# Bit patterns of each edge joined, the first weight product in quarters, residual sums on VectorE

## The reference

```python
# block 0
edge_feature = silu(edge_rbf @ We1 + be1) @ We2 + be2
msg = edge_feature * x[dst]
agg = segment_sum(msg, src, num_segments=625)
x = x + (x0 + (silu(agg @ Wn1 + bn1) @ Wn2 + bn2))   # x0 = max(layernorm(x), 0)
# block 1, on h = max(layernorm(x), 0)
h = relu(h @ W_init.T)
for l in range(3):           # mean over the edges of each node, both directions
    fwd = mean_agg(h, src, dst) @ W_fwd[l].T
    bwd = mean_agg(h, dst, src) @ W_bwd[l].T
    h = relu(concat(h, fwd, bwd) @ W_self[l].T)
# blocks 2 and 3: graph convolutions with 1/sqrt(degree) weights and dense layers
```

## Time and profile before

| | us |
|---|---|
| median of three runs | 1182.57 |
| profiled execution, its own time | 1181.72 |
| its span, first to last instruction | 1180.0 |
| PE busy | 1148.7 (97%) |
| DVE busy | 854.8 (72%) |
| ACT busy | 676.1 (57%) |
| POOL busy | 431.0 (37%) |

### The profile page before, as it was taken

How to read it: one execution, slowest core, us unless ns; L and a number is a source line. 1 busy time by engine, 2 the same in 40 slices (tenths; PEclk the granted TensorE clock), 3 DMA queues, 4 the chain that set the end, 5 groups by cost and what they waited for, 6 DMA issues and landing times.

```text
span 1180.0 us, 20814 instructions
## 1 busy us (share of the span) xinstructions
PE 1148.7 (97%) x6238; PEld 960.3 (81%) x6238; DVE 854.8 (72%) x1479; ACT 676.1 (57%) x1351; POOL 431.0 (37%) x546
## 2 busy tenths in 40 slices
PE   6999999999999999999999999999899999999998
PEld 3678887778888888888888888888879889897786
DVE  8898578877777777777777777777888325165665
ACT  3576665667667676766667676766734223141353
POOL 2002566766565655655565555553000000002000
PEclk9999999999999999999999999999999999999999
DMA  8623622222222222222222322222101203022101
GB/s 262 269 82 146 222 83 71 69 67 85 70 87 71 87 76 80 84 72 87 69 87 69 89 69 86 73 82 59 45 1 37 72 1 107 0 73 72 45 1 45
DMA packets 26966, 95.87 MB, mean 81 GB/s; under 512 B 6533, under 2 KB 6783, under 8 KB 22578
## 3 DMA queue, kind: packets, MB, share of 16 engines
q0 software_dynamic: 18592, 54.42, 15.5%
q1 hardware_dynamic: 8208, 40.84, 9.8%
q10 hardware_dynamic: 130, 0.13, 0.0%
HBM read 86.52 MB, written 8.85 MB: 81 GB/s over the span
## 4 chain that ended last, share of the span: by engine, by line
PE 74%; DVE 12%; ACT 7%; issue 4%; DMA 1%; POOL 1%; DVEq 0%; ACTq 0%; POOLq 0%
PE ps L1021 11%; PE ps L1022 11%; PE ps L1023 11%; PE ps L1014 8%; PE ps L1016 8%; PE ps L1015 8%; PE ps L1128 3%; PE ps L1127 3%; PE ps L1029 3%; PE ps L1028 3%; PE ps L1067 2%; ACT s L723 2%; PE ps L1132 2%; DVE msg L1696 1%; ACT s_hi L727 1%
## 5 line engine op out<-in xcount | busy, mean ns | idle before, releaser
L1021 PE MATMUL ps<-we_hi,s_hi 128*128 128x512 f32 x664 | 268.8, 405 | 0.0
L1022 PE MATMUL ps<-we_lo,s_hi 128*128 128x512 f32 x664 | 259.9, 391 | 0.0
L1023 PE MATMUL ps<-we_hi,s_lo 128*128 128x512 f32 x664 | 259.9, 391 | 0.0
L585 POOL DMA_INDIRECT xg<-h_dram,node_picks x166 | 177.1, 1067 | 96.2 <-POOL node_picks L575 65.6
L733 ACT ACTIVATE m_hi<-msg 128x512 fp32r<-128x512 f32 x166 | 105.0, 632 | 186.4 <-DVE msg L1696 185.0
L579 POOL DMA_INDIRECT rbf<-in_edge,edge_picks x166 | 175.1, 1055 | 50.5 <-issue 38.7
L1689 DVE TENSOR_TENSOR s_lo<-s,s_hi 128x1024 fp32r<-128x1024 f32 x83 | 101.6, 1225 | 78.3 <-ACT s_hi L727 78.3
L1701 DVE TENSOR_TENSOR m_lo<-msg,m_hi 128x512 fp32r<-128x512 f32 x166 | 114.7, 691 | 60.0 <-ACT m_hi L733 60.0
L1023 PEld LDWEIGHTS ps<-we_hi,s_lo 128*128 128x128 f32 x664 | 124.7, 188 | 27.6
L1021 PEld LDWEIGHTS ps<-we_hi,s_hi 128*128 128x128 f32 x664 | 125.0, 188 | 22.8
L1022 PEld LDWEIGHTS ps<-we_lo,s_hi 128*128 128x128 f32 x664 | 125.3, 189 | 20.6
(11 more groups left out here) (297 smaller groups left out, 2474.8 us busy)
## 6 DMA issues: line engine op xcount, KB each, us to landing
fold_dram<-folded SPq DMA_DIRECT2D x6, 1024.0 KB, 4.9
wstage<-fold_dram SPq DMA_DIRECT2D x6, 1024.0 KB, 4.8
plain<-in_fold_a SPq DMA_DIRECT2D x3, 1024.0 KB, 9.4
plain<-in_fold_b SPq DMA_DIRECT2D x3, 1024.0 KB, 11.4
stage<-in_fold_a SPq DMA_DIRECT2D x3, 1024.0 KB, 17.1
stage<-in_fold_b SPq DMA_DIRECT2D x3, 1024.0 KB, 24.3
w_raw<-in_nodew SPq DMA_DIRECT2D x3, 1024.0 KB, 10.6
wstage<-in_selfw SPq DMA_DIRECT2D x3, 1024.0 KB, 5.1
```

Source lines behind the costliest of these rows:

```text
L585: pool.indirect_dma_start(xg[t.slot][:, j], None, h_dram, bass.IndirectOffsetOnAxis(ap=node_picks[t.slot][:, j:j + 1], axis=0)).then_inc(x ...
L1021: pe.matmul(outp, lh, rh, start=False, stop=False, skip_group_check=True)
L1022: pe.matmul(outp, lh, rl, start=False, stop=False, skip_group_check=True)
L1023: return pe.matmul(outp, ll, rh, start=False, stop=False, skip_group_check=True)
```

## The change

1. *First fold.* Its factors come in four quarters of two transfers each (`quarter_in[k]`). PE starts with `first_fold()`, which goes over `k` outside and `u` inside, and makes `ranks()` after the first quarter. `AFTER` puts no group behind fold 0 and shifts the others.
2. *Bit patterns.* Edge number and the lowest bit of `dst` make one 16-bit pattern (`first_half`), `src` and the other bits of `dst` another (`second_half`). As bfloat16 numbers they multiply the one-hots, so `keyed` and its matmuls go: 12 matmuls a group. DVE makes both products for even groups and one for odd groups; for odd groups ACT makes the second by six activations 128 wide. `hot_lo`, `hot_hi`, `ended` and `ends16` are bfloat16; `iota_*`, `lo16` and `hi16` stay float16, so the comparison reads one type and writes the other. DVE gets six integer operations between counts and ranks, five operations for three ahead of `hots(0)`, and a `slot_tables()` of eleven operations for ten.
3. *Residual sums.* The ten adds move from GpSimd to DVE, between the one-hots and `s_lo`. GpSimd's `lead` falls from 14 to 2, DVE's grows from 4 to 14.
4. *H1.* The sums of both directions stand behind `turn(0)` and `turn(1)`; `adj_lo[0]` moves from ahead of the `mlp2` sums to the first of them, and the last chunk's coefficients behind `turned_lo(0)`.

```diff
-AFTER = (((), (), (0,), (1, 2, 3)), ((4, 5), (6, 7), (8, 9), (10,)), ((11, 12), (13, 14), (15, 16), (17, 18)),
...
+AFTER = (((), (), (), ()), ((0, 1), (2, 3, 4), (5, 6, 7), (8, 9)), ((10, 11), (12, 13), (14, 15), (16, 17)),
...
-H1 = woven(turn(0), turn(1), IN_DEGREES, lin(0), turn(2), lin(1), back(0), turn(3), lin(2), back(1), turn(4), lin(3), back(2),
+H1 = woven(turn(0), turn(1), ("degrees", 0, 2), ("degrees", 1, 2), lin(0), turn(2), lin(1), back(0), turn(3), lin(2), back(1), turn(4), lin(3), back(2),
...
-        hot_lo = [hot_at(f"hot_lo{i}", [EP, GROUP // 2, P, 2], F16) for i in range(HOT_RING)]
-        hot_hi = [hot_at(f"hot_hi{i}", [EP, GROUP // 2, TILES, 2], F16) for i in range(HOT_RING)]
+        hot_lo = [hot_at(f"hot_lo{i}", [EP, GROUP // 2, P, 2], BF16) for i in range(HOT_RING)]
+        hot_hi = [hot_at(f"hot_hi{i}", [EP, GROUP // 2, TILES, 2], BF16) for i in range(HOT_RING)]
...
-            load_factors(0)
+            for k in range(K):
+                for part, w in enumerate((a["fold_a"], a["fold_b"])):
+                    sp.dma_start(plain[0][:, part, k], w[0][:, k * F:k * F + F]).then_inc(quarter_in[k], 16)
...
-                pool.tensor_tensor(x_res[:, c], x_res[:, c], row_b[0:NC] if part else h32[:, c],
-                                   op=ALU.add).then_inc(res_ready, 1)
...
-            steps(pool, STEPS, step_and_residual, lead=4 + 2 * C)
+            steps(pool, STEPS, edge_step)
...
             def mark(i):
 
-                act.wait_ge(keys_ready, 1)
+                if i % ACT_EVERY == 0:
+                    return
+                act.wait_ge(ends_typed, 4)
                 act.wait_ge(hots_lo_made, i + 1)
-                for j in range(DUOS):
-                    n = i * DUOS + j
-                    act.activation(keyed[i % HOT_RING][:, j], hot_lo[i % HOT_RING][:, j], ACT.Copy,
-                                   scale=keys[:, n:n + 1].bitcast(F32)).then_inc(marks_made, 1)
+                for j in range(GROUP):
+                    n = i * GROUP + j
+                    act.activation(ended[i % HOT_RING][:, 1, j // 2, :, j % 2], hot_lo[i % HOT_RING][:, j // 2, :, j % 2],
+                                   ACT.Copy, scale=second_half[:, n:n + 1].bitcast(F32)).then_inc(marks_made, 1)
...
-                    pe.matmul(ps[:, 5, at:at + TILES], keyed[r][:, j // 2, :, j % 2], slots,
-                              start=False, stop=False, skip_group_check=True)
...
+            def first_fold():
+                for k in range(K):
+                    pe.wait_ge(quarter_in[k], 32)
+                    for u in range(K):
+                        mm = pe.matmul(ps[:, 1 + u], plain[0][:, 0, k, u * P:u * P + P], plain[0][:, 1, k],
+                                       start=k == 0, stop=k == K - 1)
+                        if k == K - 1:
+                            mm.then_inc(fold_mm, 1)
+                    if k == 0:
+                        ranks()
...
-                for v in range(2):
+                for v in range(1 if i % ACT_EVERY else 2):
                     mm = dve.tensor_tensor(ended[r][:, v], hot_lo[r][:],
...
+            def add_to_residual(t):
+                c, part = (t.c - RESIDUAL_FROM) % C, (t.c - RESIDUAL_FROM) // C
+                if part:
+                    dve.wait_ge(late_small_in, 48)
+                    dve.wait_ge(res_ready, c + 1)
+                else:
+                    dve.wait_ge(ln_act, 1 + C)
+                dve.tensor_tensor(x_res[:, c], x_res[:, c], row_b[0:NC] if part else h32[:, c],
+                                  op=ALU.add).then_inc(res_ready, 1)
...
+                if t.reg is None and RESIDUAL_FROM <= t.c < RESIDUAL_FROM + 2 * C:
+                    add_to_residual(t)
                 if t.reg is not None or t.c + 1 < STEPS:
                     silu_lo(t.at(1))
...
-            dve.wait_ge(adj_whole, 1)
-            dve.tensor_tensor(adj_lo[0][:], acc3, adj_hi[0][:], op=ALU.subtract).then_inc(adj_split, 1)
             node_weight_low(2)
...
-                    degree_rows(1, u)
+                    if c == 0:
+                        dve.wait_ge(adj_whole, 1)
+                        dve.tensor_tensor(adj_lo[0][:], acc3, adj_hi[0][:], op=ALU.subtract).then_inc(adj_split, 1)
+                    degree_rows(c, u)
```

More of the change, by code:

```diff
@@ L34 @@
 FLUSHES = 2 * STEPS - SOLO
+RESIDUAL_FROM = 4
 SOLO_BANKS = ((5, 7), (1, 2), (5, 7))
@@ L267, in build @@
         odd_i = main("odd_i", [P, TILES], I32)
-        half_i = main("half_i", [P, TILES], I32)
         loop = Region(main.at)
@@ L860, in _ @@
             copy_units("adjT", 2 * C, adjT_hi)
-            for c in range(C):
+            for c in range(C - 1):
                 deviation(1, c)
@@ L866, in _ @@
                 u = UNIT["h1"] + at
+                if (what, c) == ("degrees", 0):
+                    deviation(1, C - 1)
+                    normed(1, C - 1)
                 if what == "lin":
@@ L1133, in scatter, with ranks @@
                 mm.then_inc(scat_mm, 1)
-            pe.wait_ge(perm_zeroed, 2)
-            for m in range(FOLDS):
+            def ranks():
+                pe.wait_ge(consts_ready, 5)
+                pe.wait_ge(counts_ready, 1)
+                pe.matmul(ps[0:EP, 0, RANK_AT:RANK_AT + C], before[0:EP, 0:EP], counts32[:], start=True, stop=True).then_inc(rank_mm, 1)
+                pe.matmul(ps[:, 0, TOTAL_AT:TOTAL_AT + C], ones32[0:EP, :], counts32[:], start=True, stop=True).then_inc(rank_mm, 1)
+            def first_fold():
[8 more added lines that the diff above has]
+                        ranks()
+            first_fold()
+            pe.wait_ge(perm_zeroed, 1)
+            for m in range(1, FOLDS):
                 for u in range(K):
@@ L1620, in bucket_tables @@
                 bucket = bucket_f[len(ends) % 2]
-                link(dve.tensor_scalar(tile_base[:], bucket[:], float(NC), None, ALU.mult))
+                link(dve.tensor_scalar(tile_base[:], bucket[:], float(NC), -1.0, ALU.mult, ALU.add))
                 link(dve.tensor_copy(bucket_row[:], bucket[0:1]))
@@ L1625, in slot_tables @@
                 dve.wait_ge(perm_mm, GROUPS)
-                dve.tensor_copy(second[:], ps[:, 5, REGION:REGION + TILES]).then_inc(perm_out, 1)
-                dve.tensor_copy(slot_dst[:], ps[:, 0, 0:TILES]).then_inc(table_ready, 1)
+                for v in range(2):
+                    dve.tensor_copy(word[v][:], ps[:, 0, v * REGION:v * REGION + TILES]).then_inc(perm_out, 1)
                 dve.wait_ge(perm_out, 1)
-                dve.tensor_tensor(key[:], ps[:, 5, 0:TILES], second[:], op=ALU.add).then_inc(perm_out, 1)
@@ L1630, in slot_tables @@
-                dve.tensor_scalar(odd_slot[:], second[:], 0.0, float(-DUOS_SHIFT), ALU.is_gt, ALU.add).then_inc(perm_out, 1)
-                dve.wait_ge(perm_out, 2)
-                dve.tensor_scalar(key_p[:], key[:].bitcast(I32), KEY_SHIFT, P - 1,
+                dve.tensor_scalar(number[:], word[0][:].bitcast(I32), HALF_WORD, EDGE_BITS,
                                   ALU.logical_shift_right, ALU.bitwise_and).then_inc(perm_out, 1)
-                dve.tensor_scalar(key_t[:], key[:].bitcast(I32), KEY_SHIFT + KEY_P, None,
-                                  ALU.logical_shift_right).then_inc(perm_out, 1)
@@ L1636, in slot_tables @@
-                dve.wait_ge(perm_out, 5)
-                dve.scalar_tensor_tensor(out=number[0][:], in0=key_t[:], scalar=2.0, in1=odd_slot[:],
+                dve.tensor_scalar(odd_i[:], word[0][:].bitcast(I32), 31, None, ALU.logical_shift_right).then_inc(perm_out, 1)
+                dve.wait_ge(perm_out, 3)
+                dve.tensor_scalar(slot_edge[:], number[:], float(-EDGE_FROM), 0.0, ALU.add, ALU.max).then_inc(table_ready, 1)
+                dve.tensor_scalar(slot_q[:], word[1][:].bitcast(I32), 23, 255,
+                                  ALU.logical_shift_right, ALU.bitwise_and).then_inc(perm_out, 1)
@@ L1638, in slot_tables @@
+                dve.tensor_scalar(slot_h[:], word[1][:].bitcast(I32), 31, None, ALU.logical_shift_right).then_inc(perm_out, 1)
+                dve.tensor_scalar(slot_s[:], word[1][:].bitcast(I32), HALF_WORD, P - 1,
+                                  ALU.logical_shift_right, ALU.bitwise_and).then_inc(perm_out, 1)
+                dve.wait_ge(perm_out, 6)
+                dve.scalar_tensor_tensor(out=half_up[:], in0=slot_q[:], scalar=2.0, in1=slot_h[:],
                                          op0=ALU.mult, op1=ALU.add).then_inc(perm_out, 1)
-                dve.wait_ge(perm_out, 6)
@@ L1646, in _ @@
+                dve.tensor_scalar(slot_dst[:], dst_of[:], float(-DST_FROM), 0.0, ALU.add, ALU.max).then_inc(table_ready, 1)
             units = [(m, u) for m in range(FOLDS) for u in range(K)]
```

144 lines of the change are left out of this document (75 added, 69 removed).

## The result

The changed kernel takes 1176.12 us (median of five runs, 1173.92 to 1177.14) where the kernel before takes 1183.11 in the same comparison: ratio 0.9935, 95% interval 0.9922 to 0.9948. That is 7.0 us faster, where 16.6 were forecast, and above the range. The profiled execution took 1176.81, its span is 1175.1.

A forecast was written before the change was run, and what follows sets the result against it. TensorE, busy 1148.7 of 1180.0 us, was taken as the bound, with VectorE's chain holding the prologue. Prologue -3.4, adds -11.0 and H1 -2.2 sum to -16.6, from 1182.57 to 1166.0 us; range 1159.5 to 1174.

The forecast's parts named there:

- the prologue: Stage before the loop: VectorE's chain up to the slot tables was to get shorter, -3.4 us (-5.3 to +1).
- The adds: Ten loop steps: moving the residual adds off GpSimd takes steps from 9.39 to 8.29 us, hidden on VectorE: -11.0 us.
- H1: After the loop: lin(0) starts when the column sums end instead of waiting for ht_hi, -2.2 us (-2.4 to 0).
- What is late next is nothing but TensorE's own work: Loop: without GpSimd's adds only TensorE's work bounds a step, 8.29 us each, as it fills 564.00 of 564.00.
- ring: Prologue: VectorE's 4.5 us wait for placed groups goes, since TensorE is early, -4.5 us.
- waits for ScalarE: Prologue: VectorE's fold_lo waits about 1.0 us longer for fold_hi after each of five odd groups, +5.0 us.
- `ranks`: Prologue: standing behind the first quarter's four matmuls, it comes 1.0 us later (0 to 1.5).
- no term of the sum is one of the clock: Whole kernel: the granted clock is 1.00 in all stretches considered, so no time was put down to it.
- So the stage moves with the slot tables: End of the prologue: the second layer's start shifts as the slot tables do, with +0.35 us for their extra operation.
- TensorE as a bound: Prologue: TensorE could be 17.0 us ahead but can't use it; rival that its saving comes through whole, 1152.4, 5%.
- The marks: Prologue, odd groups: six 128-wide ScalarE activations start 0.30 us apart, 1.8 us instead of 1.2 for three 256-wide.
- the other-side rival: Prologue, hots(i) on VectorE: mixed float16 and bfloat16 comparisons run one element a cycle, total 1188.6 us; chance 10%.

The follow-up runs named there:

- Experiments 1 and 3: The changed kernel with an unused 672-byte tile put back, 1169.74 us; the kernel before with 32 unused bytes in that place, 1188.13 us.
- Experiments 5 and 12: The changed kernel with the 672-byte gap and fold 4's store held back until the first rT_hi, 1169.89 us, or the second, 1168.59 us.
- experiment 6: The changed kernel with the 672-byte gap, first factors in two transfers and ranks first again, new AFTER kept: 1172.91 us.
- experiment 7: The changed kernel with the 672-byte gap, both products of every group on VectorE and none on ScalarE: 1161.32 us, ratio 0.9816.
- experiment 4: The kernel before with only the ten residual adds moved to VectorE, leads 2 and 14: 1173.44 us, ratio 0.9915.

## Why the prediction was wrong

The sign was right and so were most of the mechanisms; the sum was more than twice too large. 16.6 was forecast, 7.0 measured. Of the 9.6 missing, 6.4 are one thing that the prediction had no term for, and 3.0 are the prologue by the landmarks. (The adds lack 0.9 and H1 0.4; together that is 1.1 more than 9.6, as landmarks are of one execution and the medians of several.)

*The step that failed* is "What is late next is nothing but TensorE's own work", with its price of 8.29 us a step: the prediction took TensorE's work in the loop as given, since no part of the change edits it. But the change removed a tile, and the price of a step rose from 8.350 to 8.433. Experiments 1 and 3 show it in both directions with nothing else changed. No row of before could show it; the line in the diff that drops `half_i` was read as nothing.

*Prologue, -3.4 forecast, -0.36 measured.* VectorE's terms held in the main: products 14 x 0.47, ring -4.3 (-4.5), waits for ScalarE +5.9 (+5.0), in all -2.53 at the slot tables (-3.75 forecast). That the one-hots came out near (+2.51 for +2.35) is luck, as two terms missed in opposite ways: `ranks` is 1.90 later, outside the 0 to 1.5 stated, and the way from there to the one-hots is 0.61 longer, where 1.35 was taken (the five operations cost 1.09 more than the three, and `ranks` itself 0.48 less at the faster pace). The prediction had "a slow first matmul" there and "no term of the sum is one of the clock"; the trace shows the first quarter's four matmuls at half the later pace. The step that failed is the one behind them, "So the stage moves with the slot tables" with +0.35 for the longer decode: from the slot tables to the second layer it is 24.58 us instead of 22.41, +2.2. TensorE being early sends the store of fold 4 into the first gather, and behind the wait the clock falls. Experiments 5 and 12 show it in one trace each: the store held back once moves the collision, held back twice takes it away and gives 4.1 us of the second layer's start, about 1.5 of them the clock's. As a gain of the whole kernel it is not shown (1.1 us in the medians, within the spread). The prediction asked what waits for TensorE, and not what TensorE's early results set off.

*TensorE as a bound.* That it has idle time in the prologue was right (13.0 us). That its early start is then worth nothing was wrong in part: undoing the quarters under the new `AFTER` costs 3.2 us (experiment 6). The row `hot_lo` with its 4.5 us said so, and the prediction used that term but not its source.

*The marks.* 0.30 from start to start was right: six take 1.90 us. That they are dear was forecast (+5.0); that the kernel is better off without them, with 6.6 us more on VectorE, was not asked. It is 8.4 us (experiment 7).

*The adds.* -11.0 forecast, -10.1 by experiment 4's steps and -9.5 by its time. The add was hidden. The base was low: 564.00 / 68 takes the steps of the window to a whole number, while TensorE's own step is 8.350. That is 0.6 of the 0.9 missing; the ten steps were also read as 9.39 from a window a little longer than they are (9.376).

*H1.* -2.2 forecast, -1.8 measured in both kernels that have it. `lin(0)` moved as forecast; both traces have the new wait of 0.63 us for `ht_hi` at a later `lin`, which the prediction had no term for.

*The types.* Mixed float16 and bfloat16 ran at 552 ns for 768 elements and 672 for 996, so the rule of the Trainium skill, page *VectorE: DVE Perf Modes*, section *What auto-detection actually checks*, held here for a tensor_tensor of two 16-bit types too; the other-side rival did not happen. Nor did the contention of the moved add with GpSimd's picks: 0.68 us.

## What to carry to other kernels

When a change adds or drops a buffer, everything behind it moves: compare the period of an untouched loop before the edits themselves are judged, and keep a gap of the old size when only the edits are to be measured. When an engine is early, the stores and loads that wait for it start early too; look at what they then meet, and check a fix at the next place as well. Work given to a second engine in small pieces costs there what stands behind it; try it on the first engine before it is split.
